# Taking a layer norm's statistics one stage earlier, in a ring of four groups, and normalising on GpSimd

## The reference, cut to what matters

```python
x = x + tanh(g_xattn[0]) * L0_xattn(layernorm(x), ctx, ctx)
x = x + tanh(g_ffn[0])   * L0_ffn(layernorm(x))          # four experts with a gate
x = x + tanh(g_xattn[1]) * L1_xattn(layernorm(x), ctx, ctx, mask)
x = x + tanh(g_ffn[1])   * L1_ffn(layernorm(x))          # the last stage

def L1_ffn(x):
    h = bit_linear(x, w1)        # x quantised per row to int8, w1 to -1, 0, 1
    h = silu(depthwise_conv1d(h))  # three taps along the sequence
    return bit_linear(h, w2)     # h quantised per row again
```

## Time and profile before

| what | value |
|---|---|
| median of 3 runs | 943.17 us (941.88 to 944.72) |
| the profiled execution, its time and its span | 943.28 us, 941.5 us |
| second attention, first maximum of scores to last | 492.5 to 753.2 us, 4.14 us a tile |
| last stage, tile 2's bias add to tile 58's | 768.19 to 918.80 us, 2.69 us a tile |
| PE, DVE, ACT, POOL busy over the span | 97%, 86%, 81%, 71% |

### The profile page before, as it was taken

The page is one execution under the profiler, slowest core; times in us unless marked ns, Lnnn a source line. Parts: engine busy times, 40 slices in busy tenths (PEclk is TensorE's granted clock), DMA queues, the critical chain, the costliest instruction groups (busy, mean ns, idle before and its releaser), DMA issues. The chain is left out here.

```text
span 941.5 us, 32708 instructions
## 1 busy us (share of the span) xinstructions
PE 913.9 (97%) x11654; PEld 737.7 (78%) x11654; DVE 810.5 (86%) x2348; ACT 763.4 (81%) x1675; POOL 664.4 (71%) x1254
## 2 busy tenths in 40 slices
PE   6999999999999999999899999999999999999996
PEld 3888888878889999998786777777777777777774
DVE  6888888899979989889788888888887869999996
ACT  5888888888887777777567787878878889999995
POOL 5787777776536556556989777676765558889883
PEclk9999999999999999999999999999999999999998
DMA  3501011100000000000000000000000003333343
GB/s 116 187 25 47 25 47 37 36 25 14 14 2 1 2 1 1 1 2 1 1 14 13 26 13 14 25 14 26 14 26 2 4 18 76 72 76 77 74 72 82
DMA packets 54272, 31.17 MB, mean 33 GB/s; under 512 B 38368, under 2 KB 46816, under 8 KB 54112
## 3 DMA queue, kind: packets, MB, share of 16 engines
q1 hardware_dynamic: 54112, 29.08, 11.9%
HBM read 16.48 MB, written 4.19 MB: 22 GB/s over the span
## 5 line engine op out<-in xcount | busy, mean ns | idle before, releaser
L997 DVE TENSOR_REDUCE smax<-score 128x16 f32<-128x1024 f32 x128 | 156.7, 1224 | 63.4 <-DVE a_st L992 38.9
L1365 PEld LDWEIGHTS bank<-vb,prob_t 128*64 128x64 f32 x4096 | 130.3, 138 | 49.8 <-issue 41.7
L1006 DVE TENSOR_TENSOR prob<-score,smax 128x512 f32<-128x512 f32 x256 | 164.9, 686 | 0.8
L642 ACT ACTIVATE prob_t<-bank 128x512 f32<-128x512 f32 x256 | 139.1, 596 | 19.8 <-PE bank L1340 5.9
L637 ACT ACTIVATE prob<-prob 128x512 f32<-128x512 f32 x256 | 147.5, 631 | 5.7 <-DVE prob L1006 5.7
L1365 PE MATMUL bank<-vb,prob_t 128*64 128x18 f32 x4096 | 142.6, 212 | 0.1
L1340 PE MATMUL bank<-const,prob 128*128 128x128 f32 x1024 | 133.1, 273 | 0.7 <-DVE x_all L1107 0.7
L1340 PEld LDWEIGHTS bank<-const,prob 128*128 128x128 f32 x1024 | 115.7, 141 | 1.6 <-DVE x_all L1107 1.1
L721 ACT ACTIVATE eb_t<-eb,gwt 128x128 f32<-128x128 f32 x256 | 81.4, 390 | 39.6 <-POOL eb_acc L494 26.0
L648 ACT ACTIVATE o_t<-bank,b_col 128x128 f32<-128x128 f32 x128 | 48.7, 380 | 66.2 <-PE bank L1340 65.9
L428 POOL TENSOR_SCALAR kj<-k_sb,const 128x512 f32<-128x512 f32 x124 | 85.2, 694 | 21.8 <-issue 21.8
(11 more groups left out here) (169 smaller groups left out, 2363.4 us busy)
## 6 DMA issues: line engine op xcount, KB each, us to landing
ctx_t<-in_ctx SPq DMA_DIRECT2D x32, 256.0 KB, 2.7
x_all<-in_x SPq DMA_DIRECT2D x16, 256.0 KB, 3.7
out_x<-x_all SPq DMA_DIRECT2D x64, 64.0 KB, 1.8
ew<-in_ew SPq DMA_DIRECT2D x2, 512.0 KB, 6.1
q2t<-q2b SPq DMA_TRANSPOSE x64, 2.5
f_cw<-in_f_cw SPq DMA_DIRECT2D x1, 768.0 KB, 7.5
w_t<-in_w_attn SPq DMA_DIRECT2D x2, 256.0 KB, 4.1
f_w<-in_f_w SPq DMA_DIRECT2D x2, 256.0 KB, 6.8
```

The lines of the kernel that those rows point to most:

```text
L642: act.activation(prob_t[:, 4 * half:4 * half + 4, :].rearrange("p i q -> p (i q)"), bank[(PT, PT2)[half]], ACT.Copy).then_inc(s["p_copied" ...
L997: dve.tensor_reduce(smax[:].rearrange("p (r h) -> p r h", r=RH), sc, AX.X, ALU.max).then_inc(s["smax_done"], 1)
L1006: dve.tensor_tensor(prob[:, par, half * 512:(half + 1) * 512].rearrange("p (r h k) -> p r h k", r=2, k=S), sc[:, g], m.unsqueeze(3).to_bro ...
L1365: last = pe.matmul(bank[OV][q, i * 2 * VW:(i + 1) * 2 * VW], prob_t[:, i, q], vb[:, k // G, v0 + b * NPAIR + i, :, :].rearrange("p h v -> ...
```

## The change

The statistics of the last stage leave it for the second attention. In DVE's attention step t of layer 1, the BN_STATS of tile t - 5 comes before the maximum of the scores, and its BN_AGGR between maximum and subtraction. They go into `ln_mv`, a ring of four groups of four tiles. The last five tiles (59 to 63) are taken in steps 2 to 6 of the last stage. POOL forms scales for a whole group (`ln_group`, four instructions) in steps 13, 17, ..., 61 of its attention, the last three groups in steps 2, 4 and 8 of the last stage, behind its xdq; scales are kept for all 64 tiles. In the last stage DVE and POOL lose their per-tile part; from tile 6 on the normalising itself is one instruction on POOL, behind xdq and behind `ln_group` where there is one. ACT loses it; tiles 0 to 5 stay with ACT at the end of the attention.

```diff
-        ln_mv = sb("ln_mv", [P, 2, 2])
-        ln_rs = sb("ln_rs", [P, 2, 1])
-        ln_nr = sb("ln_nr", [P, 2, 1])
+        ln_mv = sb("ln_mv", [P, 4, G, 2])
+        ln_nm = sb("ln_nm", [P, G])
+        ln_rs = sb("ln_rs", [P, T])
+        ln_nr = sb("ln_nr", [P, T])
...
-        def ln_rstd(pool, t, par):
-            wait(pool, "ln_mv", t + 1)
-            wait(pool, "xn_ready", t - 1)
...
+        def ln_mean_ready(dve, t):
+            if t % G == 0:
+                wait(dve, "ln_ready", LN_STEPS * (t // G - 3))
+            wait(dve, "ln", t + 1)
+        def ln_group(pool, g):
+            def stat(out, a, b, op):
+                pool.tensor_tensor(out, a, b, op).then_inc(s["ln_ready"], 1)
+            def all_tiles(c):
+                return const[:, c:c + 1].to_broadcast([P, G])
+            tiles = slice(G * g, G * (g + 1))
+            wait(pool, "ln_mv", G * (g + 1))
+            wait(pool, "ln_ready", LN_STEPS * g)
+            stat(ln_ve[:], ln_mv[:, g % 4, :, 1], all_tiles(C_EPS), ALU.add)
+            stat(ln_nm[:], ln_mv[:, g % 4, :, 0], all_tiles(C_NEG), ALU.mult)
+            wait(pool, "ln_ready", LN_STEPS * g + 2)
+            stat(ln_rs[:, tiles], ln_ve[:], all_tiles(C_POW), ALU.pow)
+            wait(pool, "ln_ready", LN_STEPS * g + 3)
+            stat(ln_nr[:, tiles], ln_nm[:], ln_rs[:, tiles], ALU.mult)
...
@@ POOL, attention step
+                    if L == 1 and j == 1 and t >= 13:
+                        ln_group(pool, (t - 13) // G)
...
@@ POOL, ffn step
-                if has(4):
-                    ln_rstd(pool, t + 4, par)
...
+                if t in (2, 4, 8):
+                    ln_group(pool, {2: NG - 3, 4: NG - 2, 8: NG - 1}[t])
+                if t >= 2 and has(4):
+                    wait(pool, "ln_ready", LN_STEPS * ((t + 4) // G + 1))
+                    wait(pool, "q1_done", t + 3)
+                    wait(pool, "xn_ready", t + 4)
+                    pool.tensor_scalar(xn[:, par, :], x_tile(t + 4), ln_rs[:, t + 4:t + 5], ln_nr[:, t + 4:t + 5],
+                                       ALU.mult, ALU.add).then_inc(s["xn_ready"], 1)
...
@@ ACT, ffn step
-                if has(4):
-                    ln_apply(act, t + 4, par, "q1_done", t + 3)
...
@@ DVE, attention step, before the maximum
+                    if L == 1 and has(-5):
+                        ln_stats(dve, t - 5)
...
@@ DVE, attention step, behind the BN_AGGR of a_mv
+                    if L == 1 and has(-5):
+                        ln_mean_ready(dve, t - 5)
+                        ln_mean(dve, t - 5)
...
@@ DVE, ffn step; likewise for the mean
-                if has(5):
-                    ln_stats(dve, t + 5, o)
+                late = T - 7 + t if 2 <= t < 7 else None
+                if late is not None:
+                    ln_stats(dve, late)
...
-                T - 7: lambda: lead_in(ffn, -5, -5), T - 6: lambda: lead_in(ffn, -4, -4),
```

More of the change, by code:

```diff
@@ L98, in build @@
         ln_st = sb("ln_st", [P, 2, 6])
-        ln_mv = sb("ln_mv", [P, 2, 2])
-        ln_ve = sb("ln_ve", [P, 2, 1])
-        ln_rs = sb("ln_rs", [P, 2, 1])
-        ln_nr = sb("ln_nr", [P, 2, 1])
+        ln_mv = sb("ln_mv", [P, 4, G, 2])
+        ln_ve = sb("ln_ve", [P, G])
+        ln_nm = sb("ln_nm", [P, G])
+        ln_rs = sb("ln_rs", [P, T])
+        ln_nr = sb("ln_nr", [P, T])
         xn = sb("xn", [P, 2, D])
@@ L241, in x_tile, with ln_stats @@
             return x_all[:, bass.ds(t * D, D)]
-        def ln_stats(dve, t, par):
+        LN_STEPS = 4
+        def ln_stats(dve, t):
             wait(dve, "x_attn", T + t + 1)
             wait(dve, "ln_mv", t - 1)
-            dve.bn_stats(ln_st[:, par, :], x_tile(t)).then_inc(s["ln"], 1)
+            dve.bn_stats(ln_st[:, t % 2, :], x_tile(t)).then_inc(s["ln"], 1)
         def ln_mean_ready(dve, t):
-            wait(dve, "ln_ready", LN_STEPS * (t - 1))
+            if t % G == 0:
+                wait(dve, "ln_ready", LN_STEPS * (t // G - 3))
@@ L252, in ln_mean_ready, with ln_mean @@
             wait(dve, "ln", t + 1)
-        def ln_mean(dve, par):
-            dve.bn_aggr(ln_mv[:, par, :], ln_st[:, par, :]).then_inc(s["ln_mv"], 1)
-        LN_STEPS = 3
-        def ln_rstd(pool, t, par):
-            wait(pool, "ln_mv", t + 1)
-            wait(pool, "xn_ready", t - 1)
[L264 to L271, removed]
+        def ln_mean(dve, t):
+            dve.bn_aggr(ln_mv[:, t // G % 4, t % G, :], ln_st[:, t % 2, :]).then_inc(s["ln_mv"], 1)
@@ L273, in ln_apply @@
         def ln_apply(act, t, par, free, free_at):
-            wait(act, "ln_ready", LN_STEPS * (t + 1))
+            wait(act, "ln_ready", LN_STEPS * (t // G + 1))
             wait(act, free, free_at)
-            act.activation(xn[:, par, :], x_tile(t), ACT.Identity, bias=ln_nr[:, par, :],
-                           scale=ln_rs[:, par, :]).then_inc(s["xn_ready"], 1)
+            act.activation(xn[:, par, :], x_tile(t), ACT.Identity, bias=ln_nr[:, t:t + 1],
+                           scale=ln_rs[:, t:t + 1]).then_inc(s["xn_ready"], 1)
@@ L617, in ffn @@
                         .then_inc(s["xq_ready"], 1)
-            lead_in(ffn, -4, -3)
+                if t in (2, 4, 8):
[6 more added lines that the diff above has]
+                                       ALU.mult, ALU.add).then_inc(s["xn_ready"], 1)
             tap_lower()
@@ L1284, in ffn @@
                         .then_inc(s["x_max"], 1)
-                if has(5):
-                    ln_mean_ready(dve, t + 5)
+                if late is not None:
+                    ln_mean_ready(dve, late)
                 if has(-1):
@@ L1292, in ffn @@
                         .then_inc(s["h_max"], 1)
-                if has(5):
-                    ln_mean(dve, o)
+                if late is not None:
+                    ln_mean(dve, late)
                 if has(0):
```

## The result

The changed kernel takes 935.85 us (median of 6; 934.3 to 938.34) against 942.63 us for the kernel before on the same chip: a ratio of 0.9926, with a 95% interval of 0.9913 to 0.9938. It is 6.8 us faster. The forecast was 1.8 us faster, in a range that ended at 937.7.

What follows compares the result with a forecast made beforehand. PE, 97% busy, bounds the kernel, waiting in the last stage for POOL's xdq. Last stage -6.1, late groups +2.7 and second attention +1.6 sum to -1.8: 943.2 to 941.4 us, range 937.7 to 945.8.

Steps and rivals of the forecast that it cites:

- 1.2 us of irregular delays: Last stage: of the 7.3 us gain over 54 tiles, 1.2 was irregular delays expected again, leaving 6.1.
- the 1.14 us taken out of POOL's step: Last stage: three small layer-norm instructions leave POOL's 2.55 us step; with the normalising added it becomes 1.8.
- PE's own work, with the chain through ACT close behind: Last stage after the change: POOL no longer binds; this does, at 2.55 us a tile.
- the wait for xdq: Last stage, sign of being right: the transpose's wait for POOL's xdq, 57 times and 24.7 us before, is nearly gone.
- The late groups: Last stage, POOL steps 2, 4 and 8: PE loses 1.1 us at each, net of an old stall 2.7 together.
- The second attention: DVE's extra BN_STATS and BN_AGGR in 59 steps cost +1.6 us; bounds 0 and 7.0.
- Another may add between 0 and 0.12: Second attention: a second BN_STATS before the maximum delays it by 0 to 0.12 us; 0.03 taken.
- the subtraction 0.02 to 0.12 late: Second attention: a second BN_AGGR between maximum and subtraction delays the subtraction by this; 0.07 us taken, upper bound 0.22.
- the four in 0.37: Four BN_AGGR in a row take 0.37 us, each further one 0.067; set against the skill's rule, which would cost 0.17.
- The normalising on POOL: Last stage: one 128x128 tensor_scalar behind xdq, 0.40 us allowed, hidden with 0.7 us to spare in a plain step.
- the rival of twice the time: Last stage: normalising on POOL takes 0.98 us, twice ACT's 0.49; group steps +1.7, in all -0.1, 943.1 us; 8%.
- the rival with cheap additions: Attention hides both added instructions (0), irregular delays go too (-7.3), groups cost 2.7: -4.6, 938.6 us; 26%.

Runs made afterwards that it cites:

- b_move_stats: Kernel before with only DVE's last-stage statistics moved into the second attention; POOL still scales tile by tile, ACT normalises: ratio 0.9928, median 936.15 us.
- a_wait_on_xdq: Changed kernel without the redundant wait for the constants in POOL's q2 and xdq of the last stage: 934.0 us, ratio 0.9911.
- b_wait_order: Kernel before with DVE's BN_STATS wait put behind those for scores and subtraction, so the maximum carries the scores' wait: ratio 0.9987, second attention 260.16 us.
- b_dummy_one: Kernel before plus one unused BN_STATS and one unused BN_AGGR per second-attention step, in 59 steps: second attention 260.74 us, j = 3 steps 3.82.
- b_dummy_three: Kernel before plus one unused BN_STATS and three unused BN_AGGR per second-attention step: second attention 262.40 us, j = 3 steps 3.95.
- a_xn_on_act: Changed kernel with the normalising back on ACT in its old place, statistics and grouped scales kept: ratio 0.9906, median 934.98 us.
- a_best: Changed kernel with late groups spread, redundant q2/xdq waits gone, waits reordered on PE and in the first attention's maximum: 931.32 us, ratio 0.9886.

## Why the prediction was wrong

By the spans of the two profiles 5.2 us were missed (-7.0 for -1.8), by the medians 5.0. The working, stretch by stretch, says +1.6 for the second attention, +2.1 for tiles 2 to 10, -5.5 for tiles 10 to 58 and nothing elsewhere.

**The last stage: right in mechanism, low in size.** The layer norm's part did hold it, and the new mean interval is 2.537 against 2.55. But I kept 1.2 us of irregular delays, on the ground that they would be the same again, and that step, "I expect the same again", failed. By the traces two of them were stops of DVE, which reached PE by way of the late mean and POOL; without POOL's wait for the mean the same kind of stop costs nothing (b_move_stats and the changed kernel alike). When POOL is full its own stops are lost instead, three in b_move_stats; in the changed kernel none shows. (The 1.2 was itself read a little high: the three intervals that repeat add up to 8.01, 2.67 a tile and not 2.66, which leaves 0.9.) With the 0.013 a tile, this is 1.7 of the miss: 7.2 gained from tile 10 to 58, where the working makes 5.5 (128.99 - 48 x 2.55 - 1.1).

**The reason given for POOL.** I put the gain down to the 1.14 us taken out of POOL's step. b_move_stats leaves it in and gets 5.1 of the 7.2. What counted was that POOL's first instruction no longer waits for DVE. The prediction named both; only a run could tell them apart. What then holds the changed kernel was half named: "PE's own work, with the chain through ACT close behind"; that chain binds every other tile (a_wait_on_xdq), so the wait for xdq was not nearly gone.

**The late groups: right.** 1.1 us each forecast, 1.06 over eight dummy groups. For tile 2 to 10 the working gives +2.1 (2.7 less 0.6 of the stage's gain), measured +1.6.

**The second attention: wrong, in sign too.** Forecast +1.6, measured -0.5: 2.1 of the miss. Two steps failed. "Another may add between 0 and 0.12": the 0.05 between the earlier trace rows was read as a price of the BN_STATS, and it was the place of a wait (b_wait_order). And the subtraction 0.02 to 0.12 late: it was 0.04 late and ended on time (the changed kernel and b_dummy_one); a loss only appears beyond the first extra BN_AGGR (b_dummy_three). The Trainium skill ("VectorE: DVE Perf Modes", The DRAIN you can't avoid) has the next operation wait until the pipe is empty, and says in the same place that one that isn't held starts earlier. The 0.065 from one BN_AGGR to the next, of 0.15 to 0.17 each, agrees with the second statement and not with the first; whether these count as held no run shows. Setting the four in 0.37 above the rule was right.

**The normalising on POOL** took 0.45, not 0.40, and was hidden in a plain step as said; in all its move gained nothing that shows (a_xn_on_act). The Trainium skill ("GPSIMD Engine Reference", Engine selection) calls one-input elementwise work roughly line-rate there. That is said against VectorE, on which no run here has this instruction, so it isn't tested; 0.45 against ACT's 0.49 is what puts the rival of twice the time out.

**The remainder.** 0.6 us lies before any edit, 0.2 behind tile 58, and 0.5 in tiles 2 to 10. The first is within what runs of one program differ by; the other two are left unexplained.

**The range** ended at 937.7 because I let no case gain in the attention, and the rival with cheap additions stopped at 0. The measurement lies 1.9 below it.

## What to carry to other kernels

Of several waits ahead of an instruction, name first the one that ends last: in these kernels it then rides on the instruction, and in a loop that binds this was worth 0.05 to 0.10 us a time, 0.6 us in the second attention and 2 to 3 us in the last stage. Look at the neighbouring stages too: in the first attention the same edit moved a delay and gave nothing. If an engine is full to the last tenth, look first for what it waits for, not for what it does: taking away one cross-engine wait gave five sevenths of the long stretch's gain with the engine's load unchanged; lightening POOL and then ACT gave the rest (1.4 and 0.7 us). A burst of 1.7 us on POOL cost PE 1.06, its length less a reserve of 0.6 to 0.7 a step; taken apart over several steps, some 0.25.

## What the runs showed of the hardware that I had not expected

- A wait on an instruction of its own ahead of the waiting one costs 0.05 us on DVE (0.85 against 0.80 behind the first score matmul), 0.07 on POOL (0.66 against 0.59 from the start of rounding) and 0.09 to 0.10 on PE (the second attention's step t = 1 from 3.87 to 3.77 in a_best).
- A BN_AGGR of 6 to 2 elements starts 0.065 us behind another. One between the maximum and the subtraction is free: the subtraction starts 1.26 behind the maximum with it and without (rows 8 and 9 of the kernel before; 708.50 and 709.76 at tile 52). A second delays its start by 0.04 but not its end.
- The time from the start to the second attention varies by 5 us (490.8 to 495.7) among the profiles. Up to 3 us of that lie between the first attention's last maximum and the second's first, and there in three clusters: 235.7 to 235.8, 237.1 to 237.3, 238.4 to 238.7. What switches between them is open.
- DVE and POOL stand still now and then for 0.2 to 0.35 us with nothing to wait for that the profile shows. The kernel before and b_wait_order, equal in the last stage, have their long intervals at the same tiles; other kernels have them elsewhere. What these stops are is open. Shown is that DVE's cost PE time only where POOL waits for DVE's mean, and that POOL's are lost where POOL is full.
